# Row transposes of a routed expert kernel: from TensorE to a DMA per tile, with the high and low parts made before the transpose

## The reference

```python
var = mean(x * x); xn = rms_w * x * rsqrt(var + 1e-6)
gate_w = softmax(xn @ wg_W + wg_b + (genre @ gg_W + gg_b))      # 8 experts
cw = the two largest of gate_w at their places, 0 elsewhere
h1 = relu(x @ W1[e] + b1[e])        # 256 -> 512
h2 = relu(h1 @ W2[e] + b2[e])       # 512 -> 512
out = x + sum over e of cw[e] * (h2 @ W3[e] + b3[e])            # 512 -> 256
```

## Time and profile before

| | before |
|---|---|
| median of 3 runs | 464.17 us |
| span of the profiled execution | 461.3 us |
| what lies around the span, to the median | 2.9 us |
| PE busy | 423.9 us (92%) |
| DVE, ACT, POOL busy | 307.7, 289.0, 305.3 us (67, 63, 66%) |
| DMA | 49.46 MB, mean 107 GB/s |
| granted TensorE clock | full in nearly all slices after the head |

### The profile page before, as it was taken

The page is one execution under the profiler, slowest core; times in us unless marked ns, Lnnn a source line. Parts: engine busy times, 40 slices in busy tenths (PEclk is TensorE's granted clock), DMA queues, the critical chain, the costliest instruction groups (busy, mean ns, idle before and its releaser), DMA issues.

```text
span 461.3 us, 13037 instructions
## 1 busy us (share of the span) xinstructions
PE 423.9 (92%) x4252; PEld 381.7 (83%) x4252; DVE 307.7 (67%) x539; ACT 289.0 (63%) x609; POOL 305.3 (66%) x457
## 2 busy tenths in 40 slices
PE   7606999999999999999999999999999999989980
PEld 6506988988999988999899999889999899979880
DVE  4799774877667577577577577555566667756650
ACT  6604949878687777787786675444444556655550
POOL 5632853778788878788778887876555666464361
PEclk9955899999999999999999999999999999999995
DMA  8989299456445434232243332342333332011231
GB/s 303 343 240 349 97 342 339 129 156 157 133 67 139 139 59 132 47 62 37 48 120 75 65 54 24 72 70 49 50 51 45 47 50 49 14 26 29 26 36 19
DMA packets 27178, 49.46 MB, mean 107 GB/s; under 512 B 8267, under 2 KB 21645, under 8 KB 24941
## 3 DMA queue, kind: packets, MB, share of 16 engines
q0 software_dynamic: 13632, 18.00, 24.0%
q1 hardware_dynamic: 9280, 30.45, 18.5%
q10 hardware_dynamic: 4205, 0.17, 0.5%
HBM read 40.08 MB, written 17.83 MB: 126 GB/s over the span
## 4 chain that ended last, share of the span: by engine, by line
PE 77%; DVE 7%; ACT 4%; DMA 2%; issue 2%; POOL 1%; another core or an unknown queue 0%; DVEq 0%; SPq 0%; POOLq 0%; ACTq 0%
PE bank L1295 51%; PE y_banks L1376 18%; PE bank L1255 3%; PE bank L1280 3%; DMA stage<-in_weights 2%; ACT area L800 2%; DVE area L1092 1%; PE bank L1164 1%; PE y_banks L1243 1%; DMA out<-area,cto 1%; DVE area L1090 1%; POOL out L638 1%; ACT area L824 1%; DVE stage L1117 1%; ACT w_hi L738 0%
## 5 line engine op out<-in xcount | busy, mean ns | idle before, releaser
L1295 PE MATMUL bank<-area,w_hi 128*128 128x256 f16 x1536 | 253.8, 273 | 0.3 <-issue 0.2
L1295 PE MATMUL bank<-area,w_lo 128*128 128x256 f16 x768 | 209.3, 273 | 0.0
L814 ACT ACTIVATE area<-bank,cprm 128x256 f32<-128x256 f32 (+1 forms) x264 | 131.0, 557 | 55.4 <-PE bank L1295 47.3
L1295 PEld LDWEIGHTS bank<-area,w_hi 128*128 (+1 forms) x1536 | 150.1, 98 | 17.9 <-issue 0.7
L638 POOL DMA_INDIRECT out<-area,cto x71 | 121.6, 1713 | 45.3 <-issue 21.0
L1090 DVE CAST area<-area 128x512 f16<-128x512 f32 (+1 forms) x144 | 68.0, 472 | 118.6 <-ACT area L814 105.7
L1092 DVE TENSOR_TENSOR area<-area 128x512 f16<-128x512 f32 (+1 forms) x144 | 100.8, 700 | 5.0
L603 POOL DMA_INDIRECT area<-x_ext,cfrom x65 | 72.0, 1107 | 37.9 <-POOL cfrom L598 27.9
L1376 PE MATMUL y_banks<-w_hi,area 128*128 (+1 forms) x520 | 90.7, 273 | 2.8 <-DVE area L1092 2.8
L1295 PEld LDWEIGHTS bank<-area,w_lo 128*128 (+1 forms) x768 | 75.1, 98 | 8.7
L824 ACT ACTIVATE area<-area,cw 128x256 f32<-128x256 f32 x71 | 32.2, 499 | 71.4 <-DVE area L1097 50.6
(11 more groups left out here) (205 smaller groups left out, 458.9 us busy)
## 6 DMA issues: line engine op xcount, KB each, us to landing
stage<-in_weights SPq DMA_DIRECT2D x10, 1024.0 KB
area<-in_x SPq DMA_DIRECT2D x8, 512.0 KB, 7.2
x_ext<-in_x SPq DMA_DIRECT2D x8, 512.0 KB
out<-in_x SPq DMA_DIRECT2D x8, 512.0 KB
w_lo<-in_weights SPq DMA_DIRECT2D x4, 1024.0 KB
w_hi<-in_weights SPq DMA_DIRECT2D x2, 1024.0 KB
out<-area,cto POOLq DMA_INDIRECT x71
area<-x_ext,cfrom POOLq DMA_INDIRECT x65
```

The lines of the kernel that those rows point to most:

```text
L814: ins = act.activation(to[:, m * T + u * wide:m * T + (u + 1) * wide], ps_h[layer][b][:, a * T + u * wide:a * T + (u + 1) * wide], ACT.Rel ...
L1295: ins = nc.tensor.matmul(banks[m // 2][:, (m % 2) * T:(m % 2) * T + wide], weight, xp[:, cols], start=(k == 0 and n == 0), stop=(k == chun ...
```

## The change

From tile 3 on (`BY_PE = 3`) the parts are made before the transpose instead of after it. `x_high(n)` reads the gathered rows in `xg` and writes the high part into `xr[:, 0]`, `x_low(n)` reads `xg` and `xr[:, 0]` and writes `xr[:, 1]`, both in the rows' own layout (a token on each partition). Then SyncE issues one DMA transpose of `xr` (128 partitions, 1024 float16 each: two parts, two halves, two chunks, 262 KB) into `xt_even` or `xt_odd`, 8 blocks of 128x128. Layer 1 waits for this DMA (`s_xt`). The parts of tile n are made in step n-3 and not in step n-2; in step 1 both tiles 3 and 4 are made. `xr` has one buffer: `x_high(n)` waits until the transpose of tile n-1 has landed. POOL's `wait_free` waits for `x_low` from tile 3 on. SyncE's list holds the weight loads between the transposes. To make room, small tensors of the head move into a part of `w_hi` that isn't filled yet (`front`).

```diff
+ROWS_AT = {1: (BY_PE, BY_PE + 1), **{i: (i + RING,) for i in range(BY_PE - 1, TILES - RING)}}
...
+        xr = sb("xr", [P, 2, SUB * H], F16)
+        xt_odd = sb("xt_odd", [P, 2, SUB * H], F16)
...
+        def xt(i):
+            return xt_even if i % 2 == 0 else xt_odd
+        def by_block(part, k):
+            return part.rearrange("p (u k t) -> p k u t", u=SUB, k=KH)[:, k]
+        def rows_of(i, a):
+            return xr[:, a, :].rearrange("p (u h) -> p u h", u=SUB)[:, 0:halves_of(i)]
...
+            def transpose_rows(i):
+                sp.wait_ge(s_xs, i + 1)
+                sp.wait_ge(s_l1, 2 * (i - 1))
+                sp.dma_start_transpose(xt(i).rearrange("p a (c t) -> p (a c) t", t=P),
+                                       xr[:, :, :].rearrange("p a c -> p (a c)")).then_inc(s_xt, 16)
...
+            for i in range(TILES):
+                for q in range(PLACES, CHUNKS):
+                    if LOAD_AT[q] == i:
+                        load(q)
+                for n in ROWS_AT.get(i, ()):
+                    transpose_rows(n)
...
-                pool.wait_ge(s_xp, i + 1)
+                pool.wait_ge(s_xp if i < BY_PE else s_xs, i + 1)
...
-                act.wait_ge(s_xp, i + 1)
-                act.activation(xt_hi, ps_x[:, :], ACT.Copy, scale=sx).then_inc(s_xhi, 1)
+                act.wait_ge(s_xg[i % RING], gathered(i) * 16)
+                if i > BY_PE:
+                    act.wait_ge(s_xt, (i - BY_PE) * 16)
+                act.activation(rows_of(i, 0), xg[:, i % RING, 0:halves_of(i), 0:H], ACT.Copy, scale=sx).then_inc(s_xhi, 1)
...
-                if next2:
-                    x_high(i + 2)
+                if i == 0:
+                    x_high(2)
+                for n in ROWS_AT.get(i, ()):
+                    x_high(n)
...
+                dve.scalar_tensor_tensor(rows_of(i, 1), xg[:, i % RING, 0:halves_of(i), 0:H], sx, rows_of(i, 0),
+                                         ALU.mult, ALU.subtract).then_inc(s_xs, 1)
...
+                came = (s_xs, i + 1) if i < BY_PE else (s_xt, (i - BY_PE + 1) * 16)
                 if i > 0:
-                    pe.wait_ge(s_xs, i + 1)
+                    pe.wait_ge(*came)
...
-                if next2 and i > 0:
-                    transpose_x(i + 2, (s + 2) % RING, turn + (s + 2) // RING + 1)
```

More of the change, by code:

```diff
@@ L94 @@
 SPAN = 2 * BATCH
+LOWS_OF = {q: i for i, q in LOWS_AT.items()}
+LOAD_AT = [None if BEFORE[q] is None or BEFORE[q] not in LOWS_OF else LOWS_OF[BEFORE[q]] + 1 for q in range(CHUNKS)]
+ROWS_AT = {1: (BY_PE, BY_PE + 1), **{i: (i + RING,) for i in range(BY_PE - 1, TILES - RING)}}
+assert sorted(n for at in ROWS_AT.values() for n in at) == list(range(BY_PE, TILES))
 EARLY = 8
@@ L189, in build_moe @@
         xg = take(RING * SUB * ROW).rearrange("p (s u h) -> p s u h", s=RING, u=SUB)
-        xt_hi, xt_lo = (take(KH * T // 2).bitcast(F16) for _ in range(2))
+        xt_even = take(KH * T).bitcast(F16).rearrange("p (a c) -> p a c", a=2)
         y32 = take(SUB * H)
@@ L399, in build_moe @@
         s_xs = sem("s_xs")
+        s_xt = sem("s_xt")
         s_l1 = sem("s_l1")
@@ L451, in b3_rows, with load @@
                   .then_inc(s_b3[e], 16)
[L453 to L466, removed]
+            def load(q):
+                e = q // 2
+                if q % 2 == 0:
+                    labels.append(sp.value_load(order[0:1, e:e + 1], min_val=0, max_val=E - 1))
+                if BEFORE[q] is not None:
+                    wait_lows(sp, max(BEFORE[q], 1))
+                sp.dma_start(staged(q), weights[bass.ds(labels[e] * 2 + q % 2, 1), :, :].rearrange("c p f -> (c p) f"))\
+                  .then_inc(s_w[PLACE[q]], 16)
+                if q % 2:
+                    b3_rows(e)
+            def transpose_rows(i):
[3 more added lines that the diff above has]
+                                       xr[:, :, :].rearrange("p a c -> p (a c)")).then_inc(s_xt, 16)
+            for q in range(2 * FRONT):
+                load(q)
+            sp.wait_ge(s_xg[1], SUB * 16)
+            for q in range(2 * FRONT, PLACES):
+                load(q)
+            copy_out(OUT_EARLY, OUT_PARTS)
+            for q in range(PLACES, CHUNKS):
+                if LOAD_AT[q] is None:
+                    load(q)
+            for i in range(TILES):
+                for q in range(PLACES, CHUNKS):
+                    if LOAD_AT[q] == i:
+                        load(q)
+                for n in ROWS_AT.get(i, ()):
+                    transpose_rows(n)
         @block.gpsimd
@@ L1127, in step @@
                     copy_weights(i + 1, 1, 1)
-                if next2:
-                    x_low(i + 2)
+                if i == 0:
+                    x_low(2)
+                for n in ROWS_AT.get(i, ()):
+                    x_low(n)
                 if next2 and i + 2 > PAIRED_AT and two(i + 2):
@@ L1281, in halves_of_layer @@
                                     banks[u][:, m * P:(m + 1) * P], own[u][(0, 0, 1)[n]][:, at_own:at_own + P],
-                                    xp[:, cols], start=(k == 0 and n == 0), stop=(k == chunks - 1 and n == 2))
+                                    chunk_of(xp, chunks, k, u), start=(k == 0 and n == 0), stop=(k == chunks - 1 and n == 2))
                     ins.then_inc(signal, 1)
@@ L1314, in layer1 @@
                     pe.wait_ge(*copied)
-                tile = (w[0], halves_of(i) * P, own and own[0], W1_AT, KH, (xt_hi, xt_lo), ps_h[0])
+                tile = (w[0], halves_of(i) * P, own and own[0], W1_AT, KH, parts, ps_h[0])
                 if i == 0:
@@ L1380, in layer3, with step @@
                             ins.then_inc(s_l3, 1)
-            def step(i, s, turn, sums=None, next1=True, next2=True):
+            def step(i, s, turn, sums=None, next1=True):
                 w = weights_at(i)
@@ L1404, in _ @@
             for i in range(TILES):
-                step(i, i % RING, i // RING, sums=SUMS_AT.get(i), next1=i + 1 < TILES, next2=i + 2 < TILES)
+                step(i, i % RING, i // RING, sums=SUMS_AT.get(i), next1=i + 1 < TILES)
 def kernel(x, cond_256, L0_cond_rms_w, L0_cond_wg_W, L0_cond_wg_b, L0_cond_gg_W, L0_cond_gg_b,
```

70 lines of the change are left out of this document (46 added, 24 removed).

## The result

The changed kernel took 469.28 us in the median of 5 runs (468.74 to 472.0), the kernel before 464.17 us (463.84 to 465.4, 5 runs): 1.0111 times as long, 95% interval 1.009 to 1.0133. It is 1.1% slower; 0.8% faster was forecast. Run again beside the kernel before on another chip, it was 1.0147 (1.0099 to 1.0194).

A forecast was written before the change was run, and what follows sets the result against it. PE was taken as the bound, POOL 0.3 us per three steps behind. Transposes removed -12.0, start stall +6.0, shared port +2.4 gave -3.6 on a 461.3 us span: 457.7, with 2.9 around it 460.6 us; range 451 to 479.

The forecast's parts named there:

- The bound before, and the tile's price: PE alone bounds about 77 to 386 us; removing four transposes saves 0.44 us a tile, 12.0 us in all.
- The rival's 11.5 tiles: Tiles on PE's path behind step 19, giving back 5.1 us in the rival with POOL as bound, chance 0.17.
- the sum: All terms together: -12.0 + 6.0 + 2.4 = -3.6 us, 460.6 us; chance of this case 0.38.
- Parts from SBUF: x_high 0.6 us and x_low 0.65 us per tile when read from SBUF; off the path, counted as nothing.
- The transpose: DMA transpose from x_low's end to landing: 5.7 us, bounds 2.7 to 10.3; hidden in steady steps below 9.2.
- The start on PE: Step 1: x_high(4) waits for tile 3's transpose, delaying PE's layer 3 of tile 2 by 6.0 us.
- The start on GpSimd: Step 1: POOL's parameter copy comes 2.5 us later, mostly absorbed by a DMA wait in step 2: +0.9 us.
- The gather due earlier: One tile in three holds ACT 3.1 us at x_high up to step 18; PE not yet held.
- The port: x_low's second SBUF input holds POOL's copies: 0.2 us a step out of 0 to 0.65, +2.4 us in all.
- POOL becomes the bound: Rival: every x_low holds POOL 0.65 us, +8.6 at step 19, 5.1 given back: +3.5, 467.7 us; chance 0.17.

The follow-up runs named there:

- e18: The changed kernel unaltered, run again beside the kernel before for a second profile: 469.59 us, 1.0147.
- e1: The changed kernel with a separate buffer for tile 4's parts, so x_high(4) doesn't wait for tile 3's transpose: 466.77 us, 1.0073.
- e3: The changed kernel with x_low reading old x in PSUM instead of gathered rows from tile 3 on, so one SBUF input: 464.69 us, 1.0021.
- e9: The changed kernel without GpSimd's copies of the index tables' columns; gathers and scatter-adds read the tables themselves: 462.06 us, 1.0001.
- e2: The changed kernel with parts of tile i+2, not i+3, made in step i, so no step makes two tiles: 459.22 us, 0.987.
- e17: The changed kernel (i+3 schedule) without GpSimd's index copies, with a separate buffer for tile 4's parts and two half-size transposes: 457.73 us, 0.9887.
- e11: The changed kernel with parts of tile i+2 in step i, two half-size transposes and no GpSimd index copies: 453.28 us, 0.9816.
- e8: The kernel before with x_low reading SBUF's ident instead of PSUM's x from tile 3 on, so two SBUF inputs: 463.57 us, 1.0007.
- e4: The kernel before with only the ten small tensors moved into w_hi's fifth expert: 464.13 us, 1.002.
- e14: e2 without GpSimd's index copies, one transpose for both parts: 458.14 us, 0.989.
- e5: The changed kernel with GpSimd's gather of tile i+5 ahead of an expert's parameters in step i: 478.76 us, 1.0329.

## Why the prediction was wrong

**The bound before, and the tile's price: right.** The late steps are 10.48 us, and steps 19 to 35 gave back 12.9 - 8.0 = 4.9 us in the first profile and 11.6 - 5.1 = 6.5 in the second. The rival's 11.5 tiles were 5.1 us; by the sum's own count they are 10.5 tiles or 4.6 us. No transposes but those of the first three tiles.

**Parts from SBUF: a little low.** x_high took 0.72 us and not 0.6, x_low 0.75 and not 0.65. It cost nothing by itself.

**The transpose: right in kind.** Its reader was released after 4.1 us at the start of the first profile, and a landing took 3.0 to 4.8 us in the second, against 5.7, in the bounds of 2.7 to 10.3. x_high waited for s_xt once. Both estimates from the Trainium skill, 1.0 us (page "DMA: Bandwidth & Descriptors", section "Latency and other measured facts") and 10.5 us (page "VectorE: DVE Perf Modes", section "The three transpose paths"), were off; eight blocks one after the other at 1.3 us each are excluded.

**The start on PE: right size, half the mechanism.** +6.0 forecast, +6.9 measured (7.5 in e18). ACT was released sooner than I thought. I had overlooked PE's wait for the weight sums, which stands ahead of layer 1 in its list, and the lower clock behind the gap. That the size came out is in part luck.

**The start on GpSimd: the step that failed.** I wrote "POOL is +0.9", having followed only `weigh(1)` to GpSimd. `weigh(2)` stands behind PE's stall, and the chain goes from PE over it to GpSimd's scatter-add. That of step 3 began at 110.37 before and at 120.61 and 117.16 in the two profiles of the changed kernel: less the head, GpSimd was 5.3 and 5.8 us late, in e1 without the stall 1.1. Part of it came from GpSimd's copies in step 2, which took up to 2.43 us; e3, without the second SBUF input, has 5.9 too.

**The gather due earlier: right on ACT, wrong behind it.** Between 137 and 272 us x_high waits for every third tile, 3.2 to 4.1 us, as I said (3.1). The sentence that failed is "Without more, PE is last and POOL costs nothing". I let POOL gain 0.2 us a step once it no longer waits. It gained nothing: from its 5.3 and 5.8 us at step 3 it came to 9.0 and 11.7 at step 19, 0.2 to 0.4 us more a step, three tiles took 33.3 to 34.0 us instead of 32.8 or less, and the chain is GpSimd's list alone. Without the second SBUF input (e3) it stayed level, 5.9 and 5.3.

**The schedule.** Between steps 2 and 18 PE's shift changed by +1.1 and +3.1 us in the changed kernel, by -2.4 in e3 and -3.2 in e9, and by -3.8 in e2, which has the same GpSimd list and the same second SBUF input. Without copies and with the split it was +0.1 for parts of tile i+3 (e17) and -7.0 for i+2 (e11), all that PE can gain. So the schedule costs as much as the port or more, though e2 also has no double step 1. Where GpSimd's list is short, the earlier due time closes a loop of one step (gather, x_high, weigh, scatter-add, next gather), and e17 against e11 shows its price, 0.7%, or 3 us. In the changed kernel itself the chain doesn't go through that loop, and why the i+3 schedule makes GpSimd's same list longer (33.3 to 34.0 us for three tiles against 32.5 to 33.2 in e2) isn't shown.

**The port: mis-sized, but less than the copies say.** I chose 0.2 us of POOL a step out of 0 to 0.65. The copies got 0.66 us longer, the upper bound, and 0.26 to 0.36 us of it reached the time. e8 shows that this is a cost only because GpSimd sets the pace. The Trainium skill's rule (page "SBUF — State Buffer", section "Who interferes with whom"), that a VectorE instruction with two SBUF inputs contends with a GpSimd instruction that reads SBUF, fits e3 and e8; what it costs depends on who is the bound.

So the rival "POOL becomes the bound", 467.7 us with a chance of 0.17, is what came. It had the right engine, but its number is near by luck: it put POOL at +0.9 and 0.45 us a step, +8.6 at step 19, and the parts were some 5.5 us and 0.2 to 0.4 a step. PE's shift at step 19 was 7.6 and 10.1 us without the head. The head adds up to 1 us that e4 can't confirm. Sum of the second profile: 1.0 (head) + 7.5 (start) + 3.1 (steps 3 to 18) - 6.5 (steps 19 to 35) = 5.1 us, the difference of the spans (466.4 - 461.3).

Open: half of what the split gains in the schedule of i+2 (e11 against e14); the schedule's effect on GpSimd's list; and the head's spread of -0.1 to 5.8 us between profiles, for which I only have that the input loads come first there.

## What to carry to other kernels

When a second engine is close behind the bound, follow a stall into its list as well, through every result that it waits for, and price each added read that can hold it and each earlier due time against that engine. Making operands earlier is not free: it takes a step from whatever produced them, and if the producer's list waits for the consumer's later work, the two are one loop, whose length counts and not the busy shares. Try another schedule before you give up the idea: one line (i+2 for i+3) turned 1.1% slower into 1.3% faster, and shorter work for GpSimd, the split and x_low's earlier place then gave 2.5%.

## What the hardware showed that I had not expected

- A transpose of 262 KB from SBUF to SBUF took 3.0 to 4.8 us from issue to landing (median 3.6, e18), one of 131 KB 2.4 to 4.6 us (median 3.1, e11): most of it doesn't go with size. SyncE was occupied for 1.2 us by most of them, of either size.
- A GpSimd operation on 128x1 elements took 3.10 us in e17 (149.96) while VectorE ran operations with two SBUF inputs each (VectorE's timeline below); the same operation took 0.31 us once in e5 (126.03):
```profile
149.85 0.74 DVE L1141 SCALAR_TENSOR_TENSOR xr<-area,small,xr 128x512 f16<-128x512 f32 x1
150.51 2.47 DVE L929 SCALAR_TENSOR_TENSOR w_lo<-stage,scale,w_hi 128x1024 f16<-128x1024 f32 x2
```
- One gap of 4.98 us on PE cost 1.7 us more behind it: 24 matmuls 4.33 us, at a granted clock of 0.59 in 95.6 to 101.0.
